# A vision tower's last sixteen tiles: another order of the tail, both states of a tile from one VectorE op, and two groups' outputs scaled by ScalarE and summed by GpSimd

## The reference

```
lu, ru, ld, rd = _shifts(x)
normed = (concat - mean) * rsqrt(var + EPS) * gamma + beta
y = conv_general_dilated(normed, W, window_strides=(8, 8)) + b      # [64, 169, 128]
h = concatenate([cls_tok, y], axis=1)
def step(S, qkv):                       # one token, all 64 images
    S = S + LR * jnp.einsum('bd,be->de', vt, kt)
    out = jnp.einsum('de,be->bd', S, qt)
h = h + attention(layernorm(h))
h = h + ffn(layernorm(h))
```

## Time and profile before

| | us |
|---|---|
| median of three runs | 229.81 (229.59 to 229.90) |
| profiled execution, whole / span of the trace | 229.93 / 228.0 |
| busy: TensorE, DVE, ACT, POOL | 199.1, 154.1, 112.0, 157.6 |
| TensorE busy in 40 to 160 us | 117.94 of 120 |
| TensorE busy in 210 to 215 us / 215 to 228 us | 3.51 of 5 / none |
| DVE busy in 210 to 215 us / 215 to 220 us | 4.62 of 5 / 4.86 of 5 |

### The profile page before, as it was taken

The page is one execution under the profiler, slowest core; times in us unless marked ns, Lnnn a source line. Parts: engine busy times, 40 slices in busy tenths (PEclk is TensorE's granted clock), DMA queues, the critical chain, the costliest instruction groups (busy, mean ns, idle before and its releaser), DMA issues.

```text
span 228.0 us, 4912 instructions
## 1 busy us (share of the span) xinstructions
PE 199.1 (87%) x1558; PEld 169.5 (74%) x1558; DVE 154.1 (68%) x760; ACT 112.0 (49%) x244; POOL 157.6 (69%) x124
## 2 busy tenths in 40 slices
PE   0299998799899999999999999999999999989400
PEld 0289896678688899888888888899888888877200
DVE  2658983351576786687777769578649866977970
ACT  6002211335334555565656585476566557587251
POOL 1049869799982899968999579579999225262130
PEclk9999999999999999999999999999999999999855
DMA  6999957912113005162062512102202220104234
GB/s 171 371 430 419 421 231 113 371 75 79 79 16 144 3 0 181 31 195 54 3 181 67 181 26 46 32 19 49 46 3 46 47 48 2 46 4 92 49 78 113
DMA packets 16543, 26.00 MB, mean 114 GB/s; under 512 B 1319, under 2 KB 13277, under 8 KB 16262
## 3 DMA queue, kind: packets, MB, share of 16 engines
q1 hardware_dynamic: 15836, 25.18, 34.7%
q10 hardware_dynamic: 682, 0.51, 0.8%
HBM read 19.77 MB, written 5.92 MB: 113 GB/s over the span
## 4 chain that ended last, share of the span: by engine, by line
PE 75%; POOL 9%; DVE 6%; DMA 4%; issue 2%; ACT 2%; SPq 0%; DVEq 0%; ACTq 0%; POOLq 0%
PE conv L462 36%; PE vr_ps L504 12%; PE first_ps L514 9%; PE outs L531 9%; POOL scaled L382 7%; PE turn L494 4%; DMA rows<-x_windows 3%; PE conv L468 2%; DVE images L818 1%; DVE state L789 1%; DVE state L797 1%; POOL g_low L1090 1%; DMA out<-images 1%; PE second_ps L603 1%; PE turn L603 1%
## 5 line engine op out<-in xcount | busy, mean ns | idle before, releaser
L462 PE MATMUL conv<-scaled,wt 128*128 128x256 f32 (+3 forms) x460 | 116.1, 373 | 9.9 <-DVE scaled L382 9.9
L382 POOL TENSOR_TENSOR scaled<-rows,gam 128x832 f32<-128x832 f32 x60 | 93.9, 1588 | 6.1 <-PE conv L462 6.1
L462 PEld LDWEIGHTS conv<-scaled,wt 128*128 128x128 f32 x460 | 77.2, 193 | 18.0 <-DMA wt<-weight 9.9
L667 ACT ACTIVATE values<-vr_ps,rstd 128x256 f32<-128x256 f32 x78 | 36.9, 474 | 65.6 <-PE vr_ps L504 55.3
L1100 POOL TENSOR_TENSOR rstd<-var,powers 128x8 f32<-128x8 f32 (+2 forms) x20 | 30.4, 1519 | 23.8 <-DVE var L809 23.8
L789 DVE TENSOR_TENSOR state<-first_ps,state 128x128 f32<-128x128 f32 x80 | 23.3, 291 | 31.2 <-PE first_ps L514 26.5
L675 ACT ACTIVATE images<-images,ln_shift,ln_gain 128x128 f32<-128x128 f32 x82 | 38.1, 484 | 7.8 <-DVE ln_shift L857 6.3
L504 PE MATMUL vr_ps<-w_high,g_low 128*128 128x256 f32 x80 | 32.4, 405 | 0.4 <-ACT values L667 0.4
L1090 POOL TENSOR_TENSOR g_low<-g_t,g_high 128x512 fp32r<-128x512 f32 x21 | 26.8, 1276 | 6.9 <-ACT g_high L654 6.9
L778 DVE BATCH_NORM_STATS2 ln_stats<-images 128x6 f32<-128x128 f32 x85 | 23.7, 284 | 6.6 <-ACT images L661 6.5
L514 PEld LDWEIGHTS first_ps<-values 64*128 64x128 f32 x160 | 19.3, 187 | 6.1 <-issue 5.9
(11 more groups left out here) (145 smaller groups left out, 235.9 us busy)
## 6 DMA issues: line engine op xcount, KB each, us to landing
rows<-x_windows SPq DMA_DIRECT2D x13, 864.0 KB, 5.8
out<-images SPq DMA_DIRECT2D x41, 128.0 KB, 2.4
images<-x_rows SPq DMA_DIRECT2D x3, 624.0 KB, 21.4
images<-x_rows SPq DMA_DIRECT2D x1, 1456.0 KB, 13.1
images<-x_rows SPq DMA_DIRECT2D x1, 1248.0 KB, 15.4
images<-x_rows SPq DMA_DIRECT2D x1, 832.0 KB, 19.2
small<-smalls SPq DMA_DIRECT2D x1, 512.0 KB, 8.6
terms<-parked SPq DMA_DIRECT2D x3, 168.0 KB
```

Source lines behind the costliest of these rows:

```text
L382: return eng.tensor_tensor(scaled[:, s, at:at + N], window, gains, ALU.mult)
L462: last = pe.matmul(conv_ps[g % 2][:, at:at + n * B], wt[:, s], scaled[:, s, a % RING:a % RING + n], start=first, stop=(g < EARLY and s == ...
L667: act.activation(values[:, t % VALUE_SLOTS].rearrange("p a e -> p (a e)"), vr_bank(t)[:, 0:2 * E], ACT.Identity, scale=rho_of(t)).then_inc ...
```

## The change

1. **Both states of a tile from one op.** For tiles 72 to 83 `pair_products` replaces `products`. The first increment is still a matmul over rows 0 to 63; the second product is taken over all 128 rows, so it is the sum of both increments. The two lie side by side in one bank (two tiles to a bank), and `pair_state` adds the state before to both halves in one 128x256 VectorE op. All four first products stand ahead of the four over 128 rows, and the semaphore rises once per two tiles.
2. **Outputs of groups 18 and 19.** ACT scales the bank into h2 (`out_copy`, eight instructions of 128x128), POOL adds h for a whole group at once (`add_outs`, two instructions of 128x512). DVE loses eight `add_out`.
3. **Order and banks.** `vr(76)` now stands ahead of the products of group 18; even tiles of the tail use bank conv1, odd ones vr_ps. DVE takes the statistics of group 18 after the states, those of group 19 and of the last tiles behind the five last `add_out`, and all these ahead of `ln2_affine(18)`. ACT moves `finish(58)` into the tail and defers tiles 61 to 71 behind the scaling of groups 18 and 19.
4. **Slots.** `H2_SLOTS` goes from 4 to 6 and `OUT_SLOTS` from 3 to 6. The first `finish` of group 21 now waits for a store of group 15, and tiles 80 to 83 for one of group 14.

```diff
-H2_SLOTS = 4
-OUT_SLOTS = 3
+H2_SLOTS = 6
+OUT_SLOTS = 6
...
+            def pair_products(g):
+                tiles = tiles_of(g)
+                pe.wait_ge(vr_ready, tile_no(tiles[-1]))
+                for t in tiles:
+                    at, slot = t % 2 * 2 * E, t % VALUE_SLOTS
+                    pe.matmul(pair_bank(t)[:, at:at + E], values[0:B, slot, 0], values[0:B, slot, 1], start=True, stop=True,
+                              skip_group_check=True)
+                for t in tiles:
+                    at, slot = t % 2 * 2 * E, t % VALUE_SLOTS
+                    last = pe.matmul(pair_bank(t)[:, at + E:at + 2 * E], values[:, slot, 0], values[:, slot, 1], start=True,
+                                     stop=True, skip_group_check=True)
+                    if t % 2:
+                        last.then_inc(pairs_done, 2)
...
+            def pair_state(t):
+                dve.wait_ge(pairs_done, 2 * ((t - TAIL) // 2 + 1))
+                dve.wait_ge(out_done, tile_no(t - STATE_SLOTS))
+                dve.wait_ge(state_ready, states_to(t - 1))
+                at = t % 2 * 2 * E
+                dve.tensor_tensor(state[:, t % STATE_SLOTS], pair_bank(t)[:, at:at + 2 * E].rearrange("p (k e) -> p k e", e=E),
+                                  state[:, (t - 1) % STATE_SLOTS, 1].unsqueeze(1).to_broadcast([P, 2, E]),
+                                  ALU.add).then_inc(state_ready, 2)
...
+            def out_copy(t):
+                g, at = t // PER_GROUP, (t % PER_GROUP) * E
+                act.wait_ge(out_done, tile_no(tiles_of(g)[-1]))
+                act.activation(tile_of(h2, H2_SLOTS, t), out_bank(g)[:, at:at + E], ACT.Identity,
+                               scale=rho_of(t)).then_inc(out_scaled, 1)
...
+            def add_outs(g):
+                pool.wait_ge(out_scaled, tiles_of(g)[-1] - TAIL + 1)
+                pool.tensor_tensor(h2[g % H2_SLOTS], h2[g % H2_SLOTS], h[g % H_SLOTS], ALU.add).then_inc(pool_h2_ready, 1)
...
+                for t in LAST_TILES:
+                    values_out(t)
+                for t in range(TAIL, TAIL + 4):
+                    out_copy(t)
+                for t in range(TAIL - 11, TAIL - 8):
+                    finish_next(t)
+                for t in range(TAIL + 4, TAIL + 8):
+                    out_copy(t)
+                for t in range(TAIL - 8, LAST_TILES[0]):
+                    finish_next(t)
...
+                add_outs(TAIL // PER_GROUP)
+                add_outs(TAIL // PER_GROUP + 1)
+                ln2_power(LAST - 2)
```

More of the change, by code:

```diff
@@ L300, in tower @@
         last_three_ready = sem("last_three_ready")
+        pairs_done = sem("pairs_done")
+        out_scaled = sem("out_scaled")
+        pool_h2_ready = sem("pool_h2_ready")
         last_stored = sem("last_stored")
@@ L324, in vr_bank @@
         def vr_bank(t):
-            return turn_ps if t >= TAIL + PER_GROUP and t % 2 else vr_ps
+            return conv_ps[1] if t >= TAIL + PER_GROUP and t % 2 == 0 else vr_ps
         def rho_of(t):
@@ L347, in banks_of, with pair_bank @@
             g = t // PER_GROUP
-            if g == LAST - 1:
-                return conv_ps[0], conv_ps[1]
-            return (turn_ps, None) if g > LAST else (first_ps, second_ps)
+            return (conv_ps[1], None) if g > LAST else (first_ps, second_ps)
+        def pair_bank(t):
+            i = (t - TAIL) // 2
+            return (first_ps, second_ps, turn_ps, conv_ps[0], first_ps, second_ps)[i]
         def ln2_col(t):
@@ L559, in tail @@
                 turn(LAST + 1)
+                vr(TAIL + 4)
                 pe.wait_ge(state_ready, states_to(TAIL - 1))
-                products(g)
-                vr(TAIL + 4)
-                pe.wait_ge(h_ready, LAST + 1)
+                pair_products(g)
                 vr(TAIL + 5)
@@ L571, in tail @@
                 pe.wait_ge(h_ready, GROUPS)
-                products(g + 1)
+                pair_products(g + 1)
                 vr(TAIL + 8)
@@ L580, in tail @@
                 pe.wait_ge(state_ready, states_to(TAIL + 3))
-                products(LAST)
+                pair_products(LAST)
                 products(LAST + 1)
@@ L707, in tail @@
             def tail():
+                values_out(TAIL + 4)
                 rows_out(LAST)
-                values_out(TAIL + 4)
-                high(LAST)
                 rows_out(LAST + 1)
                 values_out(TAIL + 5)
-                high(LAST + 1)
+                high(LAST)
                 values_out(TAIL + 6)
                 values_out(TAIL + 7)
-                for t in range(TAIL - 13, TAIL - 6):
+                high(LAST + 1)
+                for t in range(TAIL - 14, TAIL - 11):
                     finish_next(t)
@@ L719, in tail @@
                     values_out(t)
-                for t in range(TAIL - 6, LAST_TILES[0]):
+                for t in range(TAIL, TAIL + 4):
[5 more added lines that the diff above has]
+                for t in range(TAIL - 8, LAST_TILES[0]):
                     finish_next(t)
@@ L821, in ln2_stats_of @@
             def ln2_stats_of(t):
-                dve.wait_ge(h2_ready, tile_no(t))
+                if TAIL <= t < LAST_TILES[0]:
+                    dve.wait_ge(pool_h2_ready, t // PER_GROUP - TAIL // PER_GROUP + 1)
+                else:
+                    dve.wait_ge(h2_ready, tile_no(t if t < TAIL else t - 2 * PER_GROUP))
                 dve.bn_stats(ln2_stats[:, ln2_col(t)], tile_of(h2, H2_SLOTS, t)).then_inc(ln2_stats_ready, 1)
@@ L936, in tail @@
                 ln2_stats_of(TAIL - 1)
-                first_state(TAIL + 7)
                 ln2_moments(g - 1)
-                second_state(TAIL + 7)
                 ln2_variance(g - 1)
-                add_out(TAIL)
-                first_state(LAST_TILES[0])
-                add_out(TAIL + 1)
-                second_state(LAST_TILES[0])
-                add_out(TAIL + 2)
-                first_state(LAST_TILES[1])
-                add_out(TAIL + 3)
-                second_state(LAST_TILES[1])
@@ L949, in tail @@
[L949 to L956 removed]
+                pair_state(LAST_TILES[0])
+                pair_state(LAST_TILES[1])
+                pair_state(LAST_TILES[2])
+                pair_state(LAST_TILES[3])
@@ L957, in tail @@
                 ln2_affine(g - 1)
                 first_state(LAST_TILES[4])
+                group_stats(g)
                 ln2_moments(g)
                 ln2_variance(g)
-                for t in tiles_of(g + 1):
+                for t in LAST_TILES:
                     add_out(t)
@@ L966, in tail @@
                 for t in LAST_TILES:
-                    add_out(t)
+                    ln2_stats_of(t)
                 ln2_affine(g)
-                for t in LAST_TILES:
-                    ln2_stats_of(t)
                 ln2_moments(LAST)
@@ L1119, in tail @@
                 low(LAST)
-                low(LAST + 1)
                 pool.wait_ge(ln1_var_ready, LAST + 2)
                 pool.tensor_tensor(last_rstd[:], last_var[:], powers[:, 0:PER_GROUP + 1], ALU.pow).then_inc(rho_ready, 1)
-                for g in range(LAST - 3, LAST + 1):
-                    ln2_power(g)
+                low(LAST + 1)
+                ln2_power(LAST - 3)
+                add_outs(TAIL // PER_GROUP)
+                add_outs(TAIL // PER_GROUP + 1)
+                ln2_power(LAST - 2)
+                ln2_power(LAST - 1)
+                ln2_power(LAST)
             pool.memset(powers[:, 0:9], -0.5)
```

42 lines of the change are left out of this document (14 added, 28 removed).

## The result

The changed kernel takes 230.39 us (median of 12 runs, 230.20 to 230.52), the kernel before, measured beside it, 229.79 us (12 runs). The ratio is 1.0026, 95% interval 1.0018 to 1.0034: 0.60 us slower, clear of no change. The profiled execution took 230.31 us with a span of 228.5, against 229.93 and 228.0 before.

The account below looks back on a forecast made before the run. Bound in the tail: a TensorE-ACT-DVE loop, then DVE to group 18's affine, then ACT's finishes and SP's last issue. That issue moves +0.95 us, 229.93 to 230.88, forecast 230.7 from the median with gaps rounded down; range 230.0 to 231.5.

Parts of the forecast that it names:

- Products: TensorE in the tail: products no longer run beside each other, so a group takes 1.99 us instead of 1.09, +0.90.
- First pair behind the products: Delay from the start of a group's products to DVE's first paired add: 1.72 us, at group 20 1.74.
- change of height: TensorE, switch from half-height to full-height products inside a group: about 0.10 us, bounds 0 and 0.2.
- vr(76) ahead: TensorE: vr(76) placed before group 18's products delays them from 199.34 to 199.60, +0.26 us.
- DVE between: DVE from group 19's first pair through add_out(71) to group 18's reads: reads at 207.86, +1.53 us.
- States of group 20: DVE: four paired adds of 0.55 us replace 3.43 us of adds; tile 84's add at 214.63, +0.85.
- ACT and POOL: Scaling and sums of groups 18 and 19 moved off DVE stay hidden: cost 0, with 0.6 us of cover.
- Affine of group 18: DVE: this affine comes 5.36 us after tile 84's add instead of 4.45, at 219.99, +1.76.
- The end: the issues: ACT's wait for a store goes, but SP's queue of issues puts the last at 225.32 against 224.37, +0.95 us.
- 1 (no longer products): Tail products still overlap and a group stays at 1.09 us: faster, 228.8 us; chance 0.17.
- 2 (lengths cancel): Cheap paired adds, no height-change cost and vr(76) inside the wait cancel the loss: 229.9 us, no change; chance 0.17.
- 3 (POOL late): POOL's sum takes 2.5 us, making group 19 and later steps 0.6 late: 231.4 us; chance 0.08.

Follow-up runs that it names:

- the run ordered by bank: The changed kernel with both kinds of products for tiles 72 and 73 first, then for 74 and 75, and so in each group; 231.01 us.

## Why the prediction was right, step by step

The direction and the mechanism were right. The prediction had +0.9 us (229.8 to 230.7); +0.60 was measured.

- *Products.* Group 1.99 us, measured 2.00. That they run one behind the other is shown by the equal starts that vanish and come back when the pairs are undone.
- *First pair behind the products.* 1.72 and 1.74, measured 1.86 (204.37 to 206.23) and 1.89 (210.38 to 212.27). The term "change of height", 0.10, was mis-sized: it costs 0.20, the upper bound given, which the run ordered by bank measures directly. The prediction counted the one longer step behind a change and not the one at it. The Trainium skill's rule of a drain at a switch of mode (TensorEngine Tiling (Array Packing), Key Properties) agrees with that run.
- *vr(76) ahead.* +0.26, measured +0.18 (199.18 against 199.34, in an execution 0.34 ahead).
- *DVE between.* add_out(71) 0.94 behind the first pair: 0.93. Reads 0.40 behind it: 0.40. Reads to products of group 20 2.83: 2.82. From the common start of the tail the reads of group 18 are 1.57 us later, forecast 1.53.
- *States of group 20.* 2.20 us for four pairs: 2.23. Idle DVE ahead of them "over 2 us": 2.67.
- *ACT and POOL.* Cost 0, and no wait of DVE for them. 0.371 and 1.274 us were the nearest rows, 0.371 and 1.264 were measured.
- *Affine of group 18.* 5.36 us behind tile 84's add, measured 5.28.
- *The end: the issues.* SP's last four issues stand back to back, as forecast ("the store that ACT waited for is replaced by SP's own queue: +0.95"). Counted from the vr ahead of the tail, the last one starts 0.89 + 0.34 = 1.23 us later than before, 0.28 more than the sum. Of that 0.12 is already there when the finishes start (1.88 later, forecast 1.76); most of the rest is the last issue, 0.71 behind the one ahead of it instead of 0.60.
- *The end: the term that was mis-sized.* "The span ends 3.6 us later, which I leave as it is." It ended 3.24 us behind the last issue, 0.39 less than before. Two runs show that this goes with ACT's wait for a store: without it, six slots in the kernel before, 3.2 us; with it, three result slots in the changed kernel, 3.7. Nor does SP's queue alone set the end: with one issue less in it the last issue came 0.5 us earlier, and the time stayed.
- *Luck.* In the profiled executions 0.95 + 0.28 - 0.39 - 0.34 gives the 0.50 by which the spans differ. The last term, this execution's head start, has no cause that I can name, and the medians differ by 0.60. The forecast came within 0.3 us of the result in part because errors of both signs cancel.
- *Rivals.* 1 (no longer products) is refuted by the trace; 2 (lengths cancel) needed paired adds at 0.41 to 0.45, they came every 0.55; 3 (POOL late) did not occur in the changed kernel, but such a wait, 0.91 us, appeared in an experiment, from the order that the edit gave POOL and not from its speed.

The account by the runs, from 229.79 us: six slots -0.84, scaling on ACT and POOL with the rest of the order -0.68, pairs +1.50 (228.26 to 229.76), affine late +0.63; sum 230.40, measured 230.39. That it closes proves nothing, since each term is the difference of two neighbouring runs; the test is that undoing the pairs and moving the affine give 1.37 and 0.63 singly, 2.00 in all, and 2.13 together. The last two terms were measured in the other order as +1.37 and +0.76. The slots are worth 0.84 alone and 1.30 in the changed kernel, so the terms depend on the company they are in; this account holds in the order given.

## What to carry to other kernels

An op fewer on one engine can cost more upstream: the paired add needed a product over all rows, and that gave up the overlap of two half-height products, 0.9 us a group for 1.06 us of DVE time in four tiles. Count how long the producers take, and when the first piece is ready, before merging consumers. And place the op that releases another engine's long run (here an affine, and a sum on GpSimd) ahead of work that nobody waits for: two such orders were worth 0.63 and 0.97 us, more than the 0.60 that the whole rewrite moved (the second was lost and won back within the experiments).

## What the runs showed of the hardware that I had not expected

Two products on different halves of the rows overlap only when they stand close in the program: 1.10 us a group in turn, 1.64 in two runs of four, 2.00 with four over all rows. In the runs of four a pass of the second kind started ahead of three passes that the program has ahead of it, and of no more. A change between products of 64 and of 128 rows, in either direction inside a group, costs 0.20 us, as two steps of 0.10 longer than the 0.112 between passes: the one at the change and the one behind it.

And the span ends 3.2 to 3.7 us behind the last issue: 3.6 in the kernel before, with ACT's issue 0.2 us ahead of it (224.16 and 224.37), and 3.7 in the changed kernel with three result slots, also with 0.2 us (226.10 and 226.32); 3.2 in the changed kernel and in the one before with six slots, with ACT's 1.25 us ahead; and 3.6 again with POOL as third issuer. That neighbours in time lengthen it fits all of these, but no run here varied the distance alone. ACT's own issue in the kernel before:

```profile
224.16 0.74 ACTq L727 DMA_DIRECT2D out<-images  x1
```
